# A delta-rule recurrence: new order of the work around it, output stage half an iteration later, gate product on VectorE

## The reference

```python
q = silu(conv4(x @ Wq.T)); k = silu(conv4(x @ Wk.T)) * DK**-0.5; v = silu(conv4(x @ Wv.T))   # H=8, DK=64, DV=128
a = sigmoid(x @ Wa.T + ba); beta = sigmoid(x @ Wb.T + bb)
def step(S, q_t, k_t, v_t, a_t, b_t):                 # S: (batch, H, DK, DV), 1024 steps one after the other
    err = einsum('bhk,bhkv->bhv', k_t, S) - v_t
    S = a_t[:, :, None, :] * S - b_t * k_t[..., None] * err[:, :, None, :]
    return S, einsum('bhk,bhkv->bhv', q_t, S)
o = (o - mean(o)) * rsqrt(var(o) + EPS) * ln_w + ln_b
o = o * sigmoid(x @ Wg.T)
return o @ Wo.T                                       # added to x, then layer norm
```

## Time and profile before

| | |
|---|---|
| median of 3 runs | 2587.63 us (2580.47 to 2590.57) |
| the profiled execution | 2596.91 us, span of the trace 2595.2 us |
| PE busy in the span | 2262.5 us (87%) |
| VectorE (DVE) | 1451.7 us (56%) |
| ScalarE (ACT) | 1059.3 us (41%) |
| POOL | 578.5 us (22%) |
| mean granted clock of PE | 0.915 |

### The profile page before, as it was taken

The page is one execution under the profiler, slowest core; times in us unless marked ns, Lnnn a source line. Parts: engine busy times, 40 slices in busy tenths (PEclk is TensorE's granted clock), DMA queues, the critical chain, the costliest instruction groups (busy, mean ns, idle before and its releaser), DMA issues. The chain is left out here.

```text
span 2595.2 us, 45214 instructions
## 1 busy us (share of the span) xinstructions
PE 2262.5 (87%) x16525; PEld 1769.3 (68%) x16525; DVE 1451.7 (56%) x3379; ACT 1059.3 (41%) x2803; POOL 578.5 (22%) x1013
## 2 busy tenths in 40 slices
PE   4888889888888988888948799899999999969997
PEld 3777788877877887777846556555556656666675
DVE  6566666666666656666637645445545545533334
ACT  2554444554454554444422344344344444412121
POOL 6333444433344433344400000000000000000000
PEclk9899989898899988898959899989989989979999
DMA  3111111011111111111010000000000000010000
GB/s 139 33 34 34 29 27 30 18 34 34 30 30 30 26 22 34 31 29 30 13 58 1 0 1 1 2 1 1 1 2 1 1 2 1 1 66 1 1 0 16
DMA packets 76192, 54.97 MB, mean 21 GB/s; under 512 B 6200, under 2 KB 72896, under 8 KB 74944
## 3 DMA queue, kind: packets, MB, share of 16 engines
q1 hardware_dynamic: 75968, 52.04, 7.7%
HBM read 50.45 MB, written 1.57 MB: 20 GB/s over the span
## 5 line engine op out<-in xcount | busy, mean ns | idle before, releaser
L1458 DVE TENSOR_REDUCE b_nmax<-ps 128x1 f32<-128x1024 f32 (+7 forms) x256 | 193.9, 757 | 325.0 <-PE ps L1358 324.2
L1354 PE MATMUL ps<-b_kT,b_qT 64*128 64x512 f32 (+3 forms) x768 | 327.8, 535 | 17.4 <-issue 15.9
L1425 ACT ACTIVATE b_prob<-ps,b_nmax 128x1024 f32<-128x1024 f32 (+7 forms) x256 | 189.6, 740 | 334.8 <-DVE b_nmax L1458 334.7
L342 PE MATMUL ps<-xT,taps 128*128 128x128 f32 x2176 | 292.3, 278 | 0.0
L342 PEld LDWEIGHTS ps<-xT,taps 128*128 128x128 f32 x2176 | 277.1, 198 | 4.8
L828 DVE TENSOR_TENSOR prod<-ps,mt 128x128 f32<-128x128 f32 x512 | 147.4, 288 | 234.7 <-PE ps L699 171.4
L785 ACT COPY wt<-ps 32x128 f32<-32x128 f32 x512 | 129.2, 252 | 286.7 <-PE ps L688 279.4
L574 POOL TENSOR_TENSOR kfull<-kt,pair_rows 128x512 f32<-128x512 f32 x128 | 148.1, 1157 | 424.2 <-ACT kt L363 421.1
L688 PE MATMUL ps<-ident,w 128*128 128x128 f32 x512 | 169.1, 330 | 46.7 <-ACT wt L785 32.2
L1354 PEld LDWEIGHTS ps<-b_kT,b_qT 64*128 64x128 f32 x768 | 127.2, 191 | 120.1 <-issue 102.5
L1336 POOL COPY b_spread<-b_inv 128x128 f32<-128x128 f32 x128 | 37.6, 294 | 724.2 <-DVE b_inv L1478 724.2
(11 more groups left out here) (210 smaller groups left out, 4292.1 us busy)
## 6 DMA issues: line engine op xcount, KB each, us to landing
decay<-ends_dram SPq DMA_DIRECT2D x256, 128.0 KB, 5.0
wtap<-in_taps SPq DMA_DIRECT2D x4, 1024.0 KB, 11.0
f_w<-in_f_w SPq DMA_DIRECT2D x2, 2048.0 KB
f_w<-in_f_w SPq DMA_DIRECT2D x2, 768.0 KB, 5.2
xT<-in_xT SPq DMA_DIRECT2D x2, 512.0 KB, 13.7
stream<-in_x_tok SPq DMA_DIRECT2D x1, 1024.0 KB, 11.8
wkv<-in_w_kv_up SPq DMA_DIRECT2D x1, 1024.0 KB, 8.0
out<-stream SPq DMA_DIRECT2D x4, 256.0 KB, 2.5
```

The costliest lines, as they stand in the source:

```text
L342: mm = pe.matmul(part, lhsT=taps[:, tap, t * P:(t + 1) * P], rhs=xT[:, :, columns(at_next) - LOOK + tap:columns(at_next) - LOOK + tap + TS ...
L1354: mm = pe.matmul(bank[:, 0:c1 - c0], lhsT=qT[rows, f, b * T + i * P:b * T + (i + 1) * P], rhs=kT[rows, f, b * T + c0:b * T + c1], start=Tr ...
L1425: nc.scalar.activation(prob[:, u % 2, 0:n], src, ACT.Exp, bias=nmax[:, u % 4:u % 4 + 1], accum_out=total[:, w % 4, h:h + 1]).then_inc(sems ...
L1458: nc.vector.tensor_reduce(nmax[:, u % 4:u % 4 + 1], src, axis=AX.X, op=ALU.max, negate=True).then_inc(sems["max_done"], 1)
```

## The change

The list of items gets a new order; slots 4 and 5, the first two of half 1, are empty:

```diff
-        BOTH = [["a0"], ["b0", "b1"], ["a1"], ["a2", "p0"], ["b2", "b3"], ["a3", "g0"], ["g1"], ["p1", "k0.0"], ["k0.1"],
-                ["k1.0"], ["k1.1"], ["p2", "c0"], ["c1"], ["var.0"], ["var.1"], ["n0", "n1", "p3"], ["n2", "n3"],
-                ["rs0", "q0.0"], ["q0.1", "rs1"], ["p4", "q1.0"], ["q1.1"], ["v0.0"], ["v0.1"], ["p5", "v1.0"], ["v1.1"],
-                ["v2.0"], ["v2.1", "dt"], ["p6", "v3.0"], ["v3.1"], ["wo.0"], ["wo.1"], ["p7", "yt"]]
+        BOTH = [["rs0", "rs1", "k0.0"], ["k0.1"], ["k1.0"], ["k1.1", "p0"],
+                [], [], ["a0"], ["a1", "p1"],
+                ["n0", "n1"], ["wo.0"], ["wo.1", "b0", "b1"], ["a2", "p2"],
+                ["c0", "yt"], ["n2", "n3"], ["b2", "b3"], ["a3", "p3"],
+                ["c1"], ["var.0"], ["var.1", "g0"], ["g1", "p4"],
+                ["q0.0"], ["q0.1"], ["q1.0", "q1.1"], ["p5", "v0.0"],
+                ["v0.1"], ["v1.0"], ["v1.1"], ["p6", "v2.0"],
+                ["v2.1"], ["v3.0"], ["v3.1"], ["dt", "p7"]]
-        only_post = Ring([[x for x in part if x.split(".")[0] in POST] for part in BOTH], BY_DVE)
+        only_post = Ring([["rs0", "rs1", "wo.0", "wo.1", "yt"], ["g0", "g1", "c0", "c1", "var.0", "var.1"]], BY_DVE)
```

```diff
+            if q in (5, 6) and post:
+                part = slice((q - 5) * HALF, (q - 4) * HALF)
+                dve.wait_ge(S["normed"], f + 1)
+                if f:
+                    wait_kept(dve, ring, f - 1, f"g{q - 5}")
+                stt(out=cs[:, part], in0=gate[:, part], scalar=1.0, in1=cs[:, part], op0=ALU.add, op1=ALU.mult).then_inc(
+                    S["gated"], 1)
```

The products with rs stand in pieces 0 and 1 and the sum of yt in piece 13. The other pieces, with steps 7 to 11 (five instructions) now done once for all heads:

```diff
-            if 4 <= q < 12:
-                decays_piece(dve, ch, ring, f, nx, q % 4, q // 8)
-            first, second = {17: [0], 20: [1], 21: [2], 22: [3], 23: [4], 24: [5], 25: [6], 26: [7, 8]}, {
-                27: [0, 1], 28: [2], 29: [3], 30: [4, 5], 31: [6, 7, 8]}
+            decay_steps = {8: (0, 0), 9: (1, 0), 10: (2, 0), 12: (3, 0), 16: (0, 1), 17: (1, 1), 18: (2, 1), 19: (3, 1)}
+            inverse_steps = {13: [(1, 0)], 14: [(0, 0), (2, 0)], 15: [(3, 0)], 20: [(4, 0)], 21: [(5, 0)],
+                             22: [(6, 0), (0, 1)], 23: [(1, 1)], 24: [(2, 1)], 25: [(3, 1)], 26: [(4, 1), (5, 1)], 27: [(6, 1)],
+                             28: [(7, 2)], 29: [(8, 2)], 30: [(9, 2), (10, 2)], 31: [(11, 2)]}
```

ScalarE and POOL in a half:

```diff
                     ring(0)
                     keep(cc, x, 0)
+                    ring(1)
+                    if cy >= 0:
+                        keep(cy, y, 3)
+                    keep(cc, x, 1)
+                    ring(2)
+                    ring(3)
                     if cc >= 1:
                         put_back(cc - 1, x)
-                    ring(1)
+                    if j == 0:
+                        act_norm(act, both, f)
                     if j in (3, 4):
                         act_diagonal(act, f, 1 - f % 2, j - 3)
-                    if j == 5:
-                        act_norm(act, both, f)
-                    if cy >= 0:
-                        keep(cy, y, 3)
-                    ring(2)
-                    keep(cc, x, 1)
-                    ring(3)
...
-                    if j == 2:
+                    if j == 1:
                         pool_prepare(pool, both, f, nx, "near")
-                    if j == 3:
-                        pool_rstd(pool, ch, both, f)
-                        scan(ch, nc.gpsimd.tensor_tensor, f, nx)
-                    if j == 5:
-                        pool_gate(pool, ch, both, f)
-                        pool_prepare(pool, both, f, nx, 0, (S["gated"], 2 * f + 2))
-                    if j == 6:
-                        pool_prepare(pool, both, f, nx, 1, (S["k_kept"], B * pc + pb))
-                        pool_values(pool, both, f, nx, 0)
-                    if j == 7:
-                        pool_values(pool, both, f, nx, 1)
+                    if j == 5:
+                        scan(ch, nc.gpsimd.tensor_tensor, f, nx)
+                    if j == 6:
+                        pool_prepare(pool, both, f, nx, 0, (S["k_kept"], B * pc + pb))
+                        pool_prepare(pool, both, f, nx, 1)
+                        pool_rstd(pool, ch, both, f)
+                    if j == 7:
+                        pool_values(pool, both, f, nx, 0)
+                        pool_values(pool, both, f, nx, 1)
```

78 lines of the change are left out of this document (39 added, 39 removed).

## The result

| | before | after |
|---|---|---|
| median | 2584.05 us | 2482.8 us (2475.91 to 2487.36) |
| ratio, 95% interval | | 0.961 (0.957 to 0.965) |
| the profiled execution | 2596.91 us | 2482.47 us |
| mean granted clock | 0.915 | 0.933 |
| mean iteration (start of iteration 0 to that of 15) | 76.65 us | 69.34 us |

The change makes the kernel 101 us faster; 72 were predicted. The forecast was 2516 us, its range 2465 to 2590.

What follows compares the result with a forecast made beforehand. TensorE, busy 87%, bounds the kernel, with waits mainly for a late state. Iteration 66.5 + 4.7 clock + 0.3 meetings = 71.5 us, 5.15 less; x16 = -82, +10 tail and start, -72: 2516 us, range 2465 to 2590.

Steps and rivals of the forecast that it cites:

- heap of piece 31: VectorE's inverse steps at the end of half 7 delay update; PE's stall of 4 us becomes about 0.3.
- The iteration at full clock: Loop iteration, halves 0 to 7 summed without low-clock loss: 66.5 us against 71.3 before, 4.8 us better.
- POOL at nothing: POOL's moved scan, prepare and rstd cost nothing, since each half keeps room for `pool_keys`.
- Meetings of VectorE and POOL: VectorE and POOL work running side by side adds 0.3 us an iteration, bounds 0 and 1.
- Steps of the inverse: VectorE's narrow inverse steps merged at twice the width, 0.62 to 0.66 us each: 0.9 us less an iteration.
- ScalarE's order: ScalarE's late tails delay the next half's first keep; PE's waits for `wt` rise from 48 to 60 us or more.
- The clock: Low-clock cost in a loop iteration falls from 5.4 to 4.7 us, bounds 3.4 and 7.1.
- rival 1: Loop clock pays back nothing: cost 7.1 us plus one for the thin half; 2568 us, chance 0.20.
- rival 3: Clock falls in half 1 and stays low through halves 2, 3 and 4; 2627 us, slower, chance 0.08.
- Rival 2: Loop goes better: low clock costs only 1.7 us, no meetings on POOL; 2463 us, chance 0.12.
- rival 4: Something in the loop counted at nothing is late, 3 to 5 us an iteration; 2564 to 2596 us, chance 0.12.
- The tail: After the loop the rows' last stage is done twice: +9 us (7 to 10).

Runs made afterwards that it cites:

- b_spread: Kernel before with only VectorE's inverse steps spread over earlier pieces, so halves 6 and 7 end with little; 2515.8 us, ratio 0.970 to the kernel before.
- a_tail: Changed kernel with the five last inverse steps put back together in piece 31, VectorE's last of half 7; 2547.5 us, ratio 0.983 to the kernel before.
- a_rstd: Changed kernel with POOL's rstd moved from half 6 to the end of half 4; 2470.7 us, ratio 0.953 to the kernel before.
- a_nonorm: Changed kernel without ScalarE's norm, folded into VectorE's operations, POOL adding one to the gate in half 5; 2510.6 us, ratio 0.968 to the kernel before.
- a_act_old: Changed kernel with nearly ScalarE's old order: put_back behind keep 0, keep 1 behind ring 2; 2468.0 us, ratio 0.951 to the kernel before.
- a_pb: Changed kernel with put_back alone moved from the end of a half to behind keep 0; 2490.1 us, ratio 0.959 to the kernel before.
- a_diag: Changed kernel with ScalarE's diagonals at the end of halves 5 and 6 instead of 3 and 4; ratio 0.968 to the kernel before.
- a_best: Changed kernel plus filled slots, folded norm, rstd in half 4, put_back, diagonals and g0 moved, last inverse steps earlier; 2368.4 us, ratio 0.913 to before.
- a_dummy2: Changed kernel with five extra matmuls of 128 columns in half 1's empty slots, results overwritten; 2491.7 us, ratio 0.961 to the kernel before.

## Why the prediction was right, and where it was off

- **What bounds the kernel: right.** The heap of piece 31 was the costly place; the wait for `state` fell to 9.0 us (under 20 was asked for), `b_spread` takes it to 26.6 us from the side of the kernel before, and `a_tail` brings it back to 48.9.
- **The iteration at full clock: right as a sum, 66.5 us predicted, 65.97 measured.** By halves (predicted, measured): 8.2, 8.98; 7.65, 7.18; 9.0, 8.51; 7.9, 7.67; 10.0, 9.97; 8.7, 8.61; 7.7, 7.43; 7.3, 7.62. That it fits so closely is in part luck: the misses cancel. Half 0 is 0.8 longer than I had it: PE is busy 8.38 us of it where I counted 8.2, and the wait for `state` is 0.6; I had counted 0.3 of it and then left even that out of the 8.2. Half 7 holds 1.0 us of the wait for `vd` and is only 0.3 over. Halves 1 and 2 came out 0.5 better each.
- **POOL at nothing: the step that failed.** "Each half keeps room for `pool_keys`" looked at halves one by one. Scan, prepare, rstd and values now form one unbroken row, and it ends late by 1.0 us an iteration, 15.5 us in all. I had 0.2 us for a late `values`, from v3's later slot; `a_rstd` shows that this cause is worth 0.4 us and comes second.
- **Meetings of VectorE and POOL at 0.3 us: too small, and one-sided.** I looked for them at the gate's products. They are in half 7: L502 and L504 take 0.8 and 0.7 us more than their 0.64, POOL's keys and products together 1.1 us more than in `a_tail`. `update` stands behind L504, whose extra length is enough for the 0.6 us of wait for `state`, and without the meetings the wait for `vd` is 0.4 us instead of 1.0 (`a_tail`). Taking `pool_rstd` out of the row does as much to that wait, so which share of it belongs to the row's length and which to the meetings stays open.
- **Steps of the inverse.** The three wide two-input steps of 256 elements (L496 and its two neighbours) take 633, 680 and 823 ns, near the 0.62 to 0.66 I took but for the third; the last two (L502, L504) take 1463 and 1318, beside POOL's `values` (timeline above). In `a_nonorm`, where `values` comes later, the same two take 636 and 622 ns. The Trainium skill, "SBUF — State Buffer", section on who interferes with whom, says that such a VectorE instruction and a GpSimd one that reads SBUF take a shared port pair in turn. This agrees for these two steps; for the gate's `stt`, where by that rule 0.5 us more was possible, it decides nothing: L432 takes 691 ns, just its row of before (681). At the same time L488 fell from 1314 to 846 ns (L479 before). So VectorE's busy time in the loop went down by 8 us, not up by 6: a wrong sign, without weight, as place counts here and not sum.
- **ScalarE's order: half right.** The waits for `wt` were to rise from 48 us to 60 or more, in halves 1, 2 and 4. They fell to 40: L694 (L688 before) has none for `wt` left, L705 (L699) has 39.9 instead of 15.5. They are in half 1 (1.54 us an iteration), half 4 (0.72) and half 5 (0.22); half 2, for which I had 0.9 us, has none, which is its 0.5 us. The wait for the copy behind c1 fell too, from 15.7 to 10.4 us, where I had it unchanged. ScalarE's busy time fell by 15 us (20 predicted), POOL's by 27 (45 predicted, the gate alone): its products for `values` went from 1.24 to 1.59 us each, its copies went from 0.34 to 0.37 and its scan steps from 0.48 to 0.53 us.
- **The clock: the mis-sized term.** Of the 7.3 us gained in a mean iteration 5.3 are at full clock (4.8 predicted) and 2.0 the clock's. I had let its cost fall from 5.4 to 4.7, with 0.3 more for POOL; it fell to 3.4, which was my lower bound. Over 16 iterations that is 16 x (5.0 - 3.4) = 26 us, most of the 42 us by which the two profiled executions differ beyond my 72. (Part of the 5.4 belongs to the one execution profiled: it lay 12.9 us above its median, up to 0.8 us an iteration.) By halves: half 0 went from 2.3 us to 0.7 as the stand in front of it went; half 7 from 0.5 to nothing; the half with c1 and var (half 3, now half 4) only from 2.5 to 1.85; and the thin half 1, new in this, costs 1.15, of which half 2 gives 0.3 back. So both things that I weighed came true, the stand that goes by more than I gave it. What my account left out is the half with c1 and var, which ran low in all 16 iterations of before; I tied the low clock to the stand alone. The mechanism of rivals 1 and 3 was real, as the clock falls in half 1 in 13 of 16 iterations, and its price is near the 1 us of rival 1; but the rest of the cost did not stay at 7.1 us (rival 1), and half 2 ran at 1.00 in 15 of 16 iterations, where rival 3 had it low. Rival 2 had the right direction; rival 4 had the right kind, something at nothing that is late, but at 1.0 us and not 3 to 5. (The 2532 us that the prediction gives for the rule on shared ports holds its 0.3 us for meetings as well; 1 us alone makes 2527.)
- **The decay load at nothing: right.** `update` (L848) waits for no DMA in the loop, but for PE (48.6 us) and for VectorE's own L484 (2.4 us).
- **The tail: +6.0 us, +9 predicted.** From the end of the last `update` to the layer norm it is 31.1 us (25.1 before). The order of events: the second rs starts 20.6 us behind that `update`, where the only one started 13.5 us behind it, so the added stage costs 7.1, not 9.9; the projections of g and what follows partly run under it. The gate on VectorE gives back 1.2, as predicted. The start is 1.9 us longer (1.3 predicted).

The timeline of the kernel after behind the loop; both products of the gate together take 1.29 us:

```profile
1192.18 1.94 PE L311 MATMUL ps<-ident,rstd 128*128 128x128 f32 x8 [1.60 <-PEq L70]
...
1211.92 1.94 PE L311 MATMUL ps<-ident,rstd 128*128 128x128 f32 x8 [2.42 <-POOL rstd L568]
...
1215.89 1.29 DVE L432 SCALAR_TENSOR_TENSOR cs<-gate,cs 128x512 f32<-128x512 f32 x2 [1.31 <-ACT cs L518]
1217.33 3.69 PE L315 MATMUL ps<-cs,wo 128*128 128x128 f32 x16 [3.47 <-DVE cs L432]
```

**The whole.** The profiled spans differ by 114.7 us: 109.6 from iterations 0 to 14 and 11.1 from the last one, and 1.8 behind the tail, less 1.9 at the start and 6.0 in the tail. The profiled execution of before was one of its slower ones (12.9 us above its median), the one of after lies on its median; that is why the medians differ by 101.

**What stays open.** What sets the clock's pattern from one iteration to the next, why half 4 keeps its clock in `a_act_old` and not in `a_pb`, and why `a_diag` has two times. The experiments tie the clock's cost in half 0 to the long wait; what pulls it down in the half with c1 and var no run isolates.

## What to carry to other kernels

On a PE-bound loop with several engines feeding it, look first for the one heap of side work in front of a recurrent step, and count what it costs twice: once as the wait, once as the low clock behind it. Then look for the low clock half by half over the whole iteration: it fell in a second place too, where no long wait pointed to it. For an engine with a low busy share ask not how much it does but how long its longest unbroken row is, who waits for the end of it, and what runs beside that end. And judge an edit of under 1% by the stretches that ran at full clock; the total mixes it with the clock's pattern.

## What the runs showed of the hardware that I had not expected

- One wait of about 4 us an iteration costs more in clock than many of 1 us: `b_spread` has 1.2 us less at full clock, but 4.5 us less in all, and 2.7 us of wait added in `a_tail` cost 4.05 us.
- The clock also fell where PE hardly waited: in the half with c1 and var in 15 of 16 iterations of `b_spread` (one wait of 0.98 us) and in 4 of 16 of `a_best` (no wait).
- A VectorE step and a POOL product side by side both became longer: 1.46 us for L502 in the kernel after, 0.64 for the same step in `a_nonorm`; 1.59 us for POOL's L527, 1.21 in `a_tail`.
- The clock's pattern can repeat exactly: iterations of 68.2 to 68.3 us at PEclk 0.95 one after the other in `a_act_old`, `a_rstd` and `a_diag`, three kernels with different waits. It is not the same pattern: the low clock falls in halves 0 and 1 in `a_act_old` and `a_diag`, in halves 1 and 4 in `a_rstd`. One of those kernels, `a_diag`, takes 2477 us in one execution and 2509 to 2516 in five others.
- More work for PE in an idle place did not raise the mean clock (`a_dummy2`, 0.94 with and without); removing waits, and with them empty places, did (`a_best`, 0.99).
